# Two query features and one attention product moved one row block forward inside the next key projection

## What is computed

```
q, k, v = heads(xn @ Wq), heads(xn @ Wk), heads(xn @ Wv)
q_prime = relu(q @ proj);  k_prime = relu(k @ proj)       # 64 -> 256 features
kv   = einsum('bhsf,bhsd->bhfd', k_prime, v)
attn = einsum('bhsf,bhfd->bhsd', q_prime, kv) / (q_prime . sum(k_prime) + eps)
out  = attn @ Wo + bo
```

## Time and profile before

| | |
|---|---|
| median of three runs | 1494.13 us |
| the profiled execution | 1493.13 us |
| its span, first to last instruction | 1491.5 us |
| PE busy | 1415.6 us, 95% |
| DVE busy | 852.9 us, 57% |
| ACT busy | 535.4 us, 36% |
| mean granted TensorE clock | 0.982 of full |

### The profile page before, as it was taken

How to read it: one execution, slowest core, us unless ns; L and a number is a source line. 1 busy time by engine, 2 the same in 40 slices (tenths; PEclk the granted TensorE clock), 3 DMA queues, 4 the chain that set the end, 5 groups by cost and what they waited for, 6 DMA issues and landing times.

```text
span 1491.5 us, 20042 instructions
## 1 busy us (share of the span) xinstructions
PE 1415.6 (95%) x7718; PEld 1308.4 (88%) x7718; DVE 852.9 (57%) x1563; ACT 535.4 (36%) x621; POOL 184.9 (12%) x182
## 2 busy tenths in 40 slices
PE   6999899999999999999999999999999759999995
PEld 5788899999999998899999999999788658888884
DVE  7564678778778778622766233354667734433340
ACT  4333254354354354232122133322112235444441
POOL 0012210100110111000000000000001442223311
PEclk9999999999999999999999999999999869999998
DMA  9765433243233336686342033221565587877863
GB/s 310 237 157 122 78 52 78 46 83 74 50 80 74 54 80 214 229 199 166 97 125 70 29 98 103 81 77 46 165 177 146 176 218 188 221 205 181 199 151 77
DMA packets 97187, 194.34 MB, mean 130 GB/s; under 512 B 31715, under 2 KB 62426, under 8 KB 95373
## 3 DMA queue, kind: packets, MB, share of 16 engines
q1 hardware_dynamic: 76324, 145.83, 33.3%
q0 software_dynamic: 20768, 47.22, 17.4%
HBM read 129.78 MB, written 73.13 MB: 136 GB/s over the span
## 4 chain that ended last, share of the span: by engine, by line
PE 72%; DMA 14%; DVE 6%; ACT 3%; issue 2%; SPq 1%; POOL 0%; POOLq 0%; ACTq 0%; DVEq 0%
PE slot L1829 24%; PE slot L1911 12%; DMA adj_d<-stage 8%; PE slot L2057 7%; PE slot L2025 6%; PE slot L1987 5%; PE slot L1785 3%; PE kvb L2057 3%; PE kvb L1951 3%; PE slot L1771 2%; DMA adj_d<-eye_dram 2%; PE slot L2040 2%; DMA mix_d<-mixn 1%; PE slot L1936 1%; DMA dx<-x_dram 1%
## 5 line engine op out<-in xcount | busy, mean ns | idle before, releaser
L1829 PE MATMUL slot<-big_hi,slab_h 128*128 128x418 f32 x768 | 194.7, 361 | 10.8 <-DVE qp_l L1438 4.8
L1829 PE MATMUL slot<-big_lo,slab_h 128*128 128x418 f32 x768 | 189.3, 355 | 0.0
L1829 PE MATMUL slot<-big_hi,slab_l 128*128 128x418 f32 x768 | 188.2, 353 | 0.0
L1829 PEld LDWEIGHTS slot<-big_hi,slab_h 128*128 128x128 f32 x768 | 140.4, 190 | 16.6 <-DVE qp_l L1438 6.4
L1829 PEld LDWEIGHTS slot<-big_hi,slab_l 128*128 128x128 f32 x768 | 145.2, 189 | 2.3
L1829 PEld LDWEIGHTS slot<-big_lo,slab_h 128*128 128x128 f32 x768 | 145.1, 189 | 2.2
L839 POOL DMA_DIRECT2D adj_d<-stage x80 | 66.7, 834 | 484.8 <-ACT stage L919 372.3
L1911 PE MATMUL slot<-adj,xs_h 125*128 125x418 f32 x480 | 118.2, 354 | 0.8 <-DVE ztmp L1170 0.5
L1911 PE MATMUL slot<-adj,xs_l 125*128 125x418 f32 x480 | 117.4, 352 | 0.0
L1174 DVE TENSOR_SCALAR oh_src<-lane,src_lo 125x125 bf16<-125x125 f16 x320 | 84.6, 265 | 25.7 <-PE kvb L1663 18.0
L864 POOL DMA_INDIRECT list_d<-rec,spots x20 | 27.9, 1397 | 529.7 <-issue 512.4
(11 more groups left out here) (316 smaller groups left out, 2940.9 us busy)
## 6 DMA issues: line engine op xcount, KB each, us to landing
slab_raw<-slabs_dram SPq DMA_DIRECT2D x40, 512.0 KB, 4.2
ws_raw<-w_dram SPq DMA_DIRECT2D x36, 512.0 KB, 7.3
adj_d<-stage POOLq DMA_DIRECT2D x81, 117.2 KB, 3.1
w_raw<-w_dram SPq DMA_DIRECT2D x9, 1024.0 KB
adj_d<-eye_dram POOLq DMA_DIRECT2D x1, 6250.0 KB, 24.8
raw<-adj_d SPq DMA_DIRECT2D x3, 1828.8 KB
dx<-x_dram SPq DMA_DIRECT2D x10, 448.0 KB
xn_d<-dx SPq DMA_DIRECT2D x10, 448.0 KB
```

The source lines that it names most:

```text
L1829: mm = ten.matmul(ps[:, 512 * q:512 * q + CW], w[a][:, kt, :], big[b][:, kt, CW * q:CW * q + CW], start=(kt == 0 and c == 0), stop=(kt == ...
```

## The change

The four inner products of K(p+1), for p = 0 to 6, stand behind these row blocks:

| | before | after |
|---|---|---|
| QP(p,0,1) | 1 | 0, behind the transposes of S |
| AT(p,0) | 3 | 2, behind the first group |
| QP(p,1,0) | 4 | 4 |
| QP(p,1,1) | 6 | 5, behind the third group |

The list for ACT, DVE, SP and POOL, the slots, the waits and the instructions are the same ones.

```diff
                         if kt == 0:
                             kv_transposes(p)
-                        if kt == 3:
+                        if kt == 2:
                             attention_product(("AT", p, 0))
-                        feature = {1: ("QP", p, 0, 1), 4: ("QP", p, 1, 0), 6: ("QP", p, 1, 1)}.get(kt)
+                        feature = {0: ("QP", p, 0, 1), 4: ("QP", p, 1, 0), 5: ("QP", p, 1, 1)}.get(kt)
                         if feature:
                             free_slot(feature)
                             feature_product(feature, sums[SLOT[feature]])
```

## The result

The changed kernel takes 1502.71 us (median of 6 runs, 1499.77 to 1506.58) against 1493.82 us for the one before on the same chip (6 runs, 1491.46 to 1495.93). The ratio is 1.0057, 95% interval 1.0044 to 1.0070: slower by 8.5 us (6.6 to 10.5). The forecast was +8.1 us and 1502 us. Four executions of kernels in this document took 2.0 to 4.9 ms instead of 1.5 ms, and no number here uses them.

The account below looks back on a forecast made before the run. TensorE, busy for 95% of the span, was taken to bound the kernel. Per pair -0.95 + 0 + 0.48 + 0.95 + 0.68 = +1.16 us, times 7 +8.1; 1494.13 + 8.1 = 1502.2, written 1502, range 1497 to 1505.

Parts of the forecast that it names:

- The wait ahead of Q goes, -0.95: Before Q(p+1): with QP(p,1,1) behind row block 5, 4.3 us stand against 2.75 needed; -0.95 us a pair.
- QP(p,0,1) costs 0: Directly behind the transposes of S: DVE has read its slot 0.8 us earlier, so no wait; cost 0.
- AT(p,0), +0.48: One row block forward: it waits for `qp_l`, held up on DVE by the second group's operations; +0.48 us a pair.
- QP(p,1,1), +0.95: One row block forward: 2.12 us of work lie ahead of it, its slot is held 2.75; +0.95 us a pair.
- AT(p,1), which the diff does not name, +0.68: In Q(p+1): without the wait before Q, 3.85 us remain against 4.21 for the `kT` readers; +0.68 us a pair.
- Nothing is swallowed later: Behind AT(p,1): reciprocal and KK move with it, DVE's idle 1.22 us covers K's work; no change in the sum.
- The price of a restart: After any TensorE wait: starting anew adds 0.28 us as measured; by the skill page's formula, an estimated 0.15.
- the rival of the falling clock: TensorE, stopping three times a pair, loses clock (0.60 granted) once in each pair: 11 us more, 1513; 4%.
- a row block covers the eviction: Rival at QP(p,1,1): its new wait vanishes below a hold time of 2.44 us; +1.5 us, 1495.6; 5%.
- the prediction's own formula: At any TensorE wait: cost is DVE's done time minus the end of TensorE's earlier work plus 0.32; nothing where negative.
- three rivals: No new wait at QP(p,1,1): 1495.6, 5%; none at AT(p,1): 1497.5, 7%; none at AT(p,0): 1498.9, 9%.

Follow-up runs that it names:

- both products inside a row block: Kernel before, with QP(p,1,1) inside row block 6 of K(p+1) and AT(p,1) inside row block 2 of Q(p+1); ratio to before 0.9964.
- the front two alone: Kernel before, with only QP(p,0,1) and AT(p,0) moved forward, QP(p,1,1) left behind row block 6; ratio to before 1.0010.
- the exchange on DVE's list: Changed kernel, with `qp_l` of QP(p,0,1) ahead of the building of the second group on DVE; ratio to before 1.0034.
- the last feature alone: Kernel before, with only QP(p,1,1) moved, from behind row block 6 to behind row block 5; ratio to before 1.0025.
- the last feature ahead of the fourth group: Kernel before, with QP(p,1,1) still behind row block 6 but ahead of the fourth group, 0.41 us earlier; ratio to before 0.9994.

## Why the prediction was right, and where it was not

The test of the prediction is the pair, +1.14 us where +1.16 was forecast, and the list of waits, which came out place by place. That the 1502 lies within 1 us of the median is more than the method can claim: six executions of the changed kernel lie between 1499.77 and 1506.58.

- *The wait ahead of Q goes, -0.95.* Right: it is in no row after. In the kernel with both products inside a row block, where nothing takes its place, the gain was 0.93 a pair.
- *QP(p,0,1) costs 0.* Right: no wait for it in pairs 0 to 6; the front two alone cost what AT(p,0) costs.
- *AT(p,0), +0.48.* Right in size and cause. The sum of its parts was a little different: `qp_l` ended 0.15 us behind TensorE's work (0.16 forecast), TensorE answered after 0.14 instead of 0.05, and starting anew cost 0.24 instead of 0.28. Together that is 0.53, which is also what the exchange on DVE's list took off; the front two alone cost 0.48.
- *QP(p,1,1), +0.95.* Right: 0.69 idle in each pair against 0.67 forecast, and 1.41 against 1.17 for the product, 0.93 together. With the `kT` wait it makes the +0.65 of the last feature alone (0.95 + 0.68 - 0.95 = 0.68).
- *AT(p,1), which the diff does not name, +0.68.* Right: 0.40 idle and 3.71 against 3.44 are 0.67. Without this term the forecast would have been 3.4 us and outside the interval measured.
- *Nothing is swallowed later.* Right: the key-feature phase waits 3.4 us in eight places before and after.
- *The price of a restart.* The prediction took the 0.28 us that it had measured. Behind the stops ahead of features, attention products and Q it was 0.23 to 0.28 in all chains here. The 0.15 us that it had estimated besides is too small; the formula behind that estimate (the Trainium skill, page "TensorE: Matmul & The Clock Gate", section "Single matmul latency") is given for a single bf16 matmul, while the operands here are fp32r.
- *The clock.* It was granted in full from 200 to 600 us after as before, now with three short stops a pair. PE in the kernel before, then in the changed one (us, busy us, granted clock, DMA share, GB/s):

```profile
200.00:600.00 400.00, 389.74 (x2371) 1.00 0.38 84
...
200.00:600.00 400.00, 386.95 (x2344) 1.00 0.35 74
```

  So the rival of the falling clock did not come. That frequent micro-idles between matmul groups made the clock swing in one kernel (the Trainium skill, page "TensorE: Matmul & The Clock Gate", section "A second HAM failure mode: psum-queue depth-cycling") does not show here with 21 stops of 0.3 to 0.7 us in 400 us, besides those of the key-feature phase.
- *Wrong: the thresholds.* The prediction had the rival "a row block covers the eviction" decide at a hold time of 2.12 + 0.32 = 2.44 us, let AT(p,0) hang on 0.16 us, and let AT(p,1) be free with readers 0.36 us faster. By the prediction's own formula the cost is zero only at hold = cover - 0.32, so these should be 1.80, 0.48 and 0.68. The slip was in the bounds, not in the sum, and made three rivals look nearer than they were. The kernel with the last feature ahead of the fourth group brought it out.

## What to carry to other kernels

A product that passes through a shared accumulator needs a distance on both sides: what lies between it and its successor must be at least the time of the readers (with what is queued ahead of them) plus the price of a restart, 0.32 us here. Moving it forward takes from one side what it gives to the other. A wait taken out of the bounding engine's queue also brings everything behind it nearer to the work of the other engines that it needs, so look for the next consumer whose slack was smaller than that wait; it need not be in the diff.

Place such work by the instruction, not by the row block. From the same start, the whole-block moves of this change cost 8.5 us; one product 0.98 us earlier and another 0.96 us later, both inside a row block, gained 5.4 us.

## What the runs showed of the hardware

- A stop of TensorE costs more than its idle time: the product behind it takes 0.23 to 0.28 us longer, with 18 matmuls (3.67 to 3.72 against 3.44) as with 6 (1.41 against 1.17). For idle times of 0.3 to 0.7 us that is a quarter to a half of the whole price.
- Part of this price falls due without a stop: where DVE was done only 0.18 us before AT(1,1) started, its 18 matmuls took 3.57 us instead of 3.44, in the kernel with the last feature ahead of the fourth group.
- In the chains, TensorE started 0.04 us after DVE's end at the waits for the slot, but 0.14 after it ahead of AT(p,0). No run tells why.
